# One load queue, exchanged banks and a new order of work at the start of a graph-network kernel

## The reference

```python
def _L0_gnn_ref(node_features, adj_matrix, W, b):
    num_neighbours = adj_matrix.sum(axis=-1, keepdims=True)
    h = jnp.einsum('bni,io->bno', node_features, W) + b
    h = jnp.einsum('bnm,bmo->bno', adj_matrix, h)
    return h / num_neighbours
...
x = _layernorm(x + _L0_gnn_ref(x, adj, W, b), axis=-1)
x = _layernorm(x + _L1_gnn_ref(x, adj, W1, b1, W2, b2, W3, b3), axis=-1)
```

## Time and profile before

| | us |
|---|---|
| median of 3 runs | 551.27 (551.20 to 551.47) |
| profiled execution, its own time | 551.15 |
| span of that execution in the trace | 549.3 |
| what lies around the span | 1.85 |
| TensorE busy, share of the span | 537.1, 98% |
| DVE, ACT, GpSimd busy | 347.2, 306.6, 209.9 |
| start of the loop (first matmul of p5 of the first batch) | 43.71 |

### The profile page before, as it was taken

One profiled execution on the slowest core, in us unless ns is written; L12 is line 12 of the kernel. 1 busy time (PEld: TensorE's weight loads), 2 busy tenths in 40 slices (PEclk: granted clock), 3 DMA queues, 4 the chain that ended last, 5 costly groups with the idle time before them and its releaser, 6 DMA issues.

```text
span 549.3 us, 10686 instructions
## 1 busy us (share of the span) xinstructions
PE 537.1 (98%) x3695; PEld 496.8 (90%) x3695; DVE 347.2 (63%) x1032; ACT 306.6 (56%) x757; POOL 209.9 (38%) x225
## 2 busy tenths in 40 slices
PE   6899999999999999999999999999999999999996
PEld 6778998989899898998989899898998989899896
DVE  3874674756657475674756657475674756657546
ACT  4455646566555656656566555656656566554532
POOL 1954409063270814509063270814509063271100
PEclk8999999999999999999999999999999999999999
DMA  8630070511607033070511507033070521500002
GB/s 251 229 153 1 1 269 1 197 74 47 222 0 265 2 101 166 0 267 0 186 81 50 217 0 264 4 109 158 0 267 0 180 89 51 218 2 39 1 1 78
DMA packets 15286, 58.23 MB, mean 106 GB/s; under 512 B 1952, under 2 KB 2720, under 8 KB 13472
## 3 DMA queue, kind: packets, MB, share of 16 engines
q1 hardware_dynamic: 14688, 56.24, 28.4%
q10 hardware_dynamic: 576, 1.70, 0.9%
HBM read 49.55 MB, written 8.39 MB: 105 GB/s over the span
## 4 chain that ended last, share of the span: by engine, by line
PE 93%; DVE 3%; DMA 1%; ACT 1%; issue 1%; POOL 0%; SPq 0%; DVEq 0%; POOLq 0%
PE bank_a L173 16%; PE bank_a L174 16%; PE bank_a L175 16%; PE bank_b L173 15%; PE bank_b L174 15%; PE bank_b L175 15%; DMA xT_raw<-in_xT 1%; POOL adj_lo L867 0%; DVE stats L737 0%; ACT std L558 0%; DVE h_lo L637 0%; DVE xT_lo L637 0%; ACT x_hi L537 0%; DVE moments L749 0%; DVE v L730 0%
## 5 line engine op out<-in xcount | busy, mean ns | idle before, releaser
L846 POOL TENSOR_TENSOR adj_lo<-adj_raw,adj_hi 128x512 fp32r<-128x512 f32 x56 | 70.8, 1295 | 269.0 <-ACT adj_hi L459 269.0
L637 DVE TENSOR_TENSOR x_lo<-bank_a,x_hi 128x512 fp32r<-128x512 f32 x64 | 44.3, 691 | 69.5 <-ACT bank_a L539 69.5
L173 PE MATMUL bank_b<-h_hi,adj_hi 128*128 128x256 f32 (+1 forms) x272 | 75.6, 278 | 2.2 <-DVE h_lo L637 1.9
L175 PE MATMUL bank_b<-h_hi,adj_lo 128*128 128x256 f32 (+1 forms) x272 | 75.4, 277 | 0.0
L174 PE MATMUL bank_b<-h_lo,adj_hi 128*128 128x256 f32 (+1 forms) x272 | 75.4, 277 | 0.0
L514 ACT ACTIVATE std<-moments,eps_col 128x1 f32<-128x1 f32 x64 | 18.9, 295 | 95.5 <-DVE moments L707 95.5
L175 PE MATMUL bank_b<-s_hi,adj_lo 128*128 128x256 f32 x232 | 64.1, 276 | 0.0
L173 PE MATMUL bank_b<-s_hi,adj_hi 128*128 128x256 f32 x232 | 64.0, 276 | 0.0
L174 PE MATMUL bank_b<-s_lo,adj_hi 128*128 128x256 f32 x232 | 64.0, 276 | 0.0
L537 ACT ACTIVATE x_hi<-bank_a,b_col 128x512 fp32r<-128x512 f32 x64 | 43.8, 684 | 23.2 <-PE bank_a L175 22.0
L173 PEld LDWEIGHTS bank_b<-h_hi,adj_hi 128*128 128x128 f32 x272 | 51.1, 188 | 2.6 <-DVE h_lo L637 2.1
(11 more groups left out here) (109 smaller groups left out, 1632.1 us busy)
## 6 DMA issues: line engine op xcount, KB each, us to landing
adj_raw<-in_adjT SPq DMA_DIRECT2D x28, 512.0 KB, 5.4
adj_rows<-in_adj SPq DMA_DIRECT2D x14, 1024.0 KB, 9.4
out_y<-y SPq DMA_DIRECT2D x15, 512.0 KB, 2.9
xT_raw<-in_xT SPq DMA_DIRECT2D x14, 512.0 KB, 6.5
x_raw<-in_x SPq DMA_DIRECT2D x14, 512.0 KB, 7.4
w_raw<-in_w SPq DMA_DIRECT2D x4, 256.0 KB, 6.3
adj_raw<-in_adjT ACTq DMA_DIRECT2D x2, 512.0 KB, 6.6
adj_rows<-in_adjT SPq DMA_DIRECT2D x2, 512.0 KB, 5.9
```

The source lines that it names most:

```text
L173: pe.matmul(acc, st[0], mv[0], start=start, stop=False)
L175: return pe.matmul(acc, st[1], mv[0], start=False, stop=stop)
L637: return dve.tensor_tensor(lo, full, hi.bitcast(F32), ALU.subtract)
L846: pool.tensor_tensor(adj_lo[:, s, k, :], raw[:, k, :], adj_hi[:, s, k, :].bitcast(F32), ALU.subtract).then_inc(adj_split, 1)
```

## The change

Five things are done, all ahead of the loop.

1. All loads go into SP's queue, in one row and without the wait of line 199: `w0`, the halves of `xT`, the halves of the first adjacency matrix, `x`, b0, then what the second batch needs. ACT issues no transfers any more. b3 moves ahead of `w2`.
2. The first batch's p2, p3 and p4 write to banks `bank_b`, and the second batch's p1 to `bank_a`, which is the reverse of before. So the second batch's p1 no longer waits for the first batch's `v1`.
3. TensorE does the first quarter of p2 of the first batch (k = 0, 6 of 24 matmuls) ahead of tile 0 of the second batch's p1, not behind it; and that tile waits for the second batch's `h` and adjacency parts one k at a time, not for all four.
4. GpSimd makes `x1_lo` of tiles 0, 1 and 2 of the first batch; DVE makes only that of tile 3. They lie between GpSimd's other work.
5. ACT and DVE work in another order: ACT begins the second adjacency matrix ahead of the first `std1`, DVE splits `xT` of the second batch ahead of `norm1`, and does three turns of `norm1` ahead of the second batch's `h_lo`.

```diff
+        def bank_g(batch):
+            return bank_b[0:2] if batch is FIRST else bank_a[2:4]
+        def bank_x2(batch):
+            return bank_b[2:4] if batch is FIRST else bank_a[0:2]
+        def bank_s2(batch):
+            return bank_b if batch is FIRST else bank_a
+        def bank_v1(batch):
+            return bank_a if batch is second else bank_b
...
-            sp.wait_ge(adj_loaded[1], DMA)
+            for half in range(2):
+                tiles = half_of(half, T)
+                sp.dma_start(adj_raw[:, tiles, :], adjT[0, :, tiles, :]).then_inc(adj_loaded[half], DMA)
+            sp.dma_start(x_raw[:, :, :], x[0]).then_inc(x_loaded, DMA)
+            sp.dma_start(b0_all[:, :], b0.partition_broadcast(P)).then_inc(b_loaded[0], DMA)
             sp.dma_start(xT1_raw[:, :, :], xT[1]).then_inc(xT_loaded, DMA)
...
-            def p2_first():
-                for k in range(T):
-                    pe.wait_ge(x1_split, k + 1)
+            def p2_first(tiles):
+                for k in tiles:
+                    if k < T - 1:
+                        pe.wait_ge(x1_first_split, k + 1)
+                    else:
+                        pe.wait_ge(x1_split, T)
...
-                pe.wait_ge(h_split, at(new, T, T))
-                pe.wait_ge(adj_split, at(new, T, T))
+                if new is not second:
+                    pe.wait_ge(h_split, at(new, T, T))
+                    pe.wait_ge(adj_split, at(new, T, T))
...
-                    if new is second:
-                        pe.wait_ge(v1_ready, j + 1)
...
                     for k in range(T):
+                        if new is second and j == 0:
+                            pe.wait_ge(h_split, at(new, T, k + 1))
+                            pe.wait_ge(adj_split, at(new, T, k + 1))
...
+            p2_first(range(0, 1))
             p1(second, range(0, 1))
-            p2_first()
+            p2_first(range(1, T))
             p1(second, range(1, 2))
...
-            norm1(FIRST, range(0, 1))
             split_xT(second, 0)
             split_xT(second, 1)
-            norm1(FIRST, range(1, 2))
+            norm1(FIRST, range(0, 3))
             h(second, bank_a)
-            norm1(FIRST, range(2, T + 2))
+            norm1(FIRST, range(3, T + 2))
```

93 lines of the change are left out of this document (53 added, 40 removed).

## The result

| | before | after |
|---|---|---|
| median of 5 runs | 551.27 (550.59 to 551.47) | 548.95 (548.42 to 549.95) |
| ratio of the runs | | 0.9963, 95% interval 0.9948 to 0.9977 |
| profiled execution, its own time | 551.15 | 549.95 |
| span of that execution | 549.3 | 548.1 |
| start of the loop in it | 43.71 | 42.62 |

The change is worth 2.3 us by these medians, where 4.3 were forecast (two later groups of runs give 1.35 and 1.6). The time lies inside the range (545.4 to 549.5), but in the part of it that belonged to rival (b). The profiled execution of the changed kernel is the slowest of its five, so its trace shows a gain of 1.2 us and not of 2.3.

The account below looks back on a forecast made before the run. TensorE alone bounds the loop, so only the loop's start can move. Gains of 2.6 + 1.1 + 1.8 us, less 0.2 for hand-overs and 1.0 for GpSimd and DVE slowing each other, gave 4.3: 546.9 us, range 545.4 to 549.5.

Parts of the forecast that it names:

- rival (b): Loads ahead of the loop: single queue delivers less than two did, 250 GB/s all through; 549.3 us; chance 0.26.
- The bound and the loop: From 43.7 us on TensorE alone bounds, unchanged; only a shift of the loop's start shifts the end.
- Part 1: Loads in one queue, up to p0 of the second batch: that starts at 16.1, not 18.70; 2.6 us gained.
- With the same sum of bytes over time: First loads: one queue moves bytes at the old summed rate, so the matrix's first half lands at 7.7 us.
- a landing comes some 0.9 us behind its last byte: First loads: lag from byte count to landing, estimated from x landing at 10.5 us, used to time the one queue.
- Parts 2 to 5, the wait ahead of p2: TensorE between second batch's p0 and first batch's p2: idle 0.95 us where it had 2.07; 1.1 us gained.
- Parts 2 to 5, p2 in 7.2 us instead of 8.95: From p2's start to its end: shorter mostly because the low clock goes; 1.8 us gained.
- The rest: From p2's end to the loop (p3, p4, three tiles of p1, 11.14 us before): nothing gained.
- The worry about p4 and `w_lo`: Ahead of p4: GpSimd's last weight part ends near 33.9, p4 at 34.1 to 34.3; any further lateness reaches the end.
- the 0.2 set aside for hand-overs: Whole walk to the loop: 0.2 us taken off the 5.5 us of gains, putting the loop's start at 38.4.
- The allowance of 1.0: Whole walk to the loop: 1.0 us taken off because GpSimd and DVE slow each other, leaving a 4.3 us gain.
- the prediction's own sign of being wrong: Second batch's loads: forecast counts as wrong if xT of the second batch lands behind 14 us.

Follow-up runs that it names:

- the kernel with `norm1` ahead: Changed kernel with one turn of the first batch's norm1 on DVE put back ahead of the second batch's xT splits; 549.90 us, ratio 0.9974.
- one queue alone: Kernel before with only its loads changed: all in SP's queue without the wait, order of work and banks as before; 550.15 us, ratio 0.9981.

## Why the prediction failed

**The bound and the loop**: right. Nothing changed behind the loop's start, and the run times follow that moment to 0.2 us. The direction was right too; the size was about twice what was measured.

**Part 1, 2.6 us forecast; 0.6 in the profiled execution, 1.0 for the loads alone by the medians.** This is the step that failed. It took the first product right (5.68 for 5.8) and from the first `adj_hi` on it was right too: that copy came 1.96 us later than forecast (9.66 for 7.7), and p0 of the second batch 1.97 us later (18.07 for 16.1). What failed is the landing, for two reasons of about the ratio one to two. "With the same sum of bytes over time" did not hold: the slices of after reach 1.31 MB at 7.5 us, where those of before do at 6.8 (0.7 us). And "a landing comes some 0.9 us behind its last byte" did not hold: ACT has the first half of the matrix 2.2 us behind that sum (7.5 to 9.66), the second half of `xT` 2.4 us (5.5 to 7.85), `xT` of the second batch 2.0 us (12.1 to 14.1). The 0.9 was read off `x`, the last but one of a row of loads behind which the queue ran dry. With more loads queued behind it the sum of bytes did not tell when a load was complete. Either part of the bytes counted by then belonged to later loads, or the end of a load was reported later while the queue was busy; the traces don't tell these two apart. The Trainium skill (DMA: Bandwidth & Descriptors, section Queues, rings and completion order) says that one transfer is split over up to sixteen engines, each with its own ring, and that transfers of one issuing engine need not complete in their order; a lag like this one would fit, but no run here shows it engine by engine.

How little the one queue gave the matrix is seen on ACT before:

```profile
9.64 0.63 ACT L459 ACTIVATE xT_hi<-xT_raw 128x512 fp32r<-128x512 f32 x1 [1.67 <-DMA xT_raw<-in_xT]
10.17 0.61 ACT L459 ACTIVATE adj_hi<-adj_raw 128x512 fp32r<-128x512 f32 x1
```

There the first `adj_hi` came at 10.17 only because it stood behind the second half of `xT`; all of the matrix had landed by 9.14, when SP's wait for it was over the earlier trace rows. In the one queue `xT` came 1.8 us sooner (7.85 for 9.64), but even the first half of the matrix later than the whole of it before (9.66), and 0.5 us was left.

**Parts 2 to 5, the wait ahead of p2: 1.1 us forecast, nothing measured.** From p0 of the second batch to the next product it is 4.91 us (18.07 to 22.98) where it was 4.92 (18.70 to 23.62). GpSimd is the releaser, as said. Its chain from the end of the low part of tile 2 to the end of the first `x1_lo` is 9.4 us (13.5 to 22.9), forecast 8.15: the `xb` are 0.9 longer, and 0.5 is a wait for ACT (other rows give 0.15 back). The forecast named the mutual slowing and took 1.0 off at the end for it; it did not see that `adj_hi` behind a waiting `std1` on ACT, which it had found in before, stays in the new order one place further on (18.59). DVE's and ACT's part of the chain is nearly as late as GpSimd's, as the kernel with `norm1` ahead shows: with GpSimd relieved, ACT's `x1_hi` is the last.

**Parts 2 to 5, p2 in 7.2 us instead of 8.95: 1.8 forecast, 0.9 measured** (22.98 to 31.0 is 8.0). This step failed as well. The reason given, 1.6 us of low clock, was wrong. The low clock is gone, but it had cost nothing: behind it stood DVE's `x1_lo`, and at full clock the waits come to light (0.55 and 0.53 in one queue alone). The clock's loss and the engines' lateness lay over one another, and the sum counted the first as if it lay bare. In the changed kernel the second place is the third `x1_lo`, 0.52 where 0.2 to 0.3 was forecast.

**The rest, "nothing": 0.5 us slower.** p3 waits 0.56 for `g_lo`: on ACT a `std1` of the second batch, itself waiting 3.12 us for DVE, stands ahead of `g_hi`. In before `g_lo` ended at 34.09, just ahead of p3's start at 34.23, and the listing shows no wait. The worry about p4 and `w_lo` did not come true: p4 waits 0.73 for DVE's `x_lo`, as before.

**Sum.** The walk had the loop at 38.4, the trace has it at 42.62, 4.2 us later: 3.15 up to the first `x1_lo`, 0.8 in p2 and 0.5 behind it, less the 0.2 set aside for hand-overs. The allowance of 1.0 covered a quarter of that, which leaves 3.2. This trace is the slowest of its five; the median's loop would start near 41.6.

**Rival (b)** came nearest: `xT` of the second batch behind 14 (14.1, which is also the prediction's own sign of being wrong), near 2 us idle ahead of p2, and a fitting time, 549.3. Its mechanism was right only in part. The rate was not 250 GB/s all through: it was low up to 6.7 us, yet the stretches from 5.6 to 12 and from 12 to 18 us have 340 and 390, and much of the delay lay between the bytes and the landings. GpSimd did wait for ACT, but because ACT's copy stood behind a `std1`; in (b) ACT waits for the second adjacency matrix, which it did not. So part of the agreement in time is luck. It was given 0.26 because the rate had passed 400 GB/s near 8 us in before; the queue reaches 400 here as well.

## What to carry to other kernels

When loads are put into one queue, don't time them by the sum of bytes: with more loads queued behind, the second half of `xT` and the first half of the matrix landed 1.4 to 2.5 us behind their byte count here, and from one execution to the next the landing moved by over a microsecond. Before a stretch of low clock (or any slow stretch) is booked as a gain, look at which engine's result is next due behind it: 3.2 us at half speed were worth nothing in the kernel before, since the waits took their place, and a similar stretch cost over a microsecond (an estimate) where the results were already there. And a version that looks better on one chip by about the spread of its executions has to run beside its rival on one chip before its mechanism is believed.
